# Layer-0 quantised network: its inner half one round later, its first product a round ahead of the gelu, and the bias product over 128 rows

## The reference, cut to what matters

```python
def act_quant(x):
    scale = 127.0 / jnp.clip(jnp.max(jnp.abs(x), axis=-1, keepdims=True), 1e-05)
    q = jnp.clip(jnp.round(x * scale), -128.0, 127.0) / scale
    ...
def bitlinear(x, w, b):
    xq = act_quant(rmsnorm(x))
    wq = weight_quant(w)
    return jnp.einsum('bsd,fd->bsf', xq, wq) + b
h = bitlinear(x, w1, b1)                 # 128 -> 512
h = jax.nn.gelu(h, approximate=False)
return bitlinear(h, w2, b2)              # 512 -> 128
...
x = x + _L0_ffn_ref(_layernorm(x, axis=-1), L0_ffn_w1, L0_ffn_b1, L0_ffn_w2, L0_ffn_b2)
```

## Time and profile before

| | before |
|---|---|
| median of 3 runs | 3581.4 us (3580.28 to 3582.94) |
| the profiled execution | 3559.48 us, its span 3557.9 us |
| mean granted TensorE clock | 0.859 |
| busy share: PE, DVE, ACT, POOL | 79%, 63%, 34%, 12% |
| L601, the bias product: MATMULs, busy, mean of one | 128, 132.6 us, 1137 ns |
| idle time of ACT ahead of the gelu (L639), ended by L601 | 131.5 us in 64 waits |

### The profile page before, as it was taken

How to read it: one execution, slowest core, us unless ns; L and a number is a source line. 1 busy time by engine, 2 the same in 40 slices (tenths; PEclk the granted TensorE clock), 3 DMA queues, 4 the chain that set the end, 5 groups by cost and what they waited for, 6 DMA issues and landing times. The chain is left out here.

```text
span 3557.9 us, 66932 instructions
## 1 busy us (share of the span) xinstructions
PE 2806.2 (79%) x24556; PEld 1846.6 (52%) x24556; DVE 2226.2 (63%) x5515; ACT 1219.6 (34%) x1872; POOL 433.6 (12%) x748
## 2 busy tenths in 40 slices
PE   5867769995999999999987888799852676885356
PEld 4623325663666666666545555466541564664126
DVE  6765548995355555555546777777014557997668
ACT  4535548883000000000016566455320113442230
POOL 0011110000000000000000000034033003442003
PEclk9955559997999999999988888899975778997568
DMA  2010000002121212121200000010322220000001
GB/s 83 27 54 1 1 10 17 15 12 96 60 84 53 91 48 95 48 95 48 95 8 16 10 9 9 2 41 27 90 65 61 60 53 3 0 0 7 0 0 47
DMA packets 88409, 136.96 MB, mean 38 GB/s; under 512 B 42949, under 2 KB 54597, under 8 KB 87242
## 3 DMA queue, kind: packets, MB, share of 16 engines
q1 hardware_dynamic: 80746, 114.75, 10.2%
q0 software_dynamic: 7520, 20.34, 1.9%
HBM read 117.75 MB, written 17.30 MB: 38 GB/s over the span
## 5 line engine op out<-in xcount | busy, mean ns | idle before, releaser
L1424 PE MATMUL banks<-l1f_xe,l1f_w 128*128 128x512 f32 x1024 | 486.7, 598 | 11.1 <-DVE l1f_xe L1623 11.1
L1623 DVE TENSOR_TENSOR l1f_xe<-l1f_hT,l1f_rwb 128x512 f32<-128x512 f32 x256 | 173.3, 692 | 301.0 <-PE banks L1426 278.2
L1426 PEld LDWEIGHTS banks<-l1f_w,l1f_xe 128*128 128x128 f32 x2048 | 269.5, 192 | 123.5 <-issue 123.5
L1629 DVE TENSOR_TENSOR l1f_ae<-l1f_aoT,l1f_rwb 128x512 f32<-128x512 f32 x256 | 172.7, 690 | 160.3 <-PE banks L1454 156.1
L1426 PE MATMUL banks<-l1f_w,l1f_xe 128*128 128x128 f32 x2048 | 270.2, 275 | 0.0
L1424 PEld LDWEIGHTS banks<-l1f_xe,l1f_w 128*128 128x128 f32 x1024 | 176.9, 192 | 141.8 <-issue 127.5
L1454 PE MATMUL banks<-l1f_ae,l1f_w 128*128 128x512 f32 x512 | 225.3, 598 | 1.4 <-DVE l1f_ae L1629 1.4
L1454 PEld LDWEIGHTS banks<-l1f_ae,l1f_w 128*128 128x128 f32 x512 | 97.1, 192 | 118.3 <-issue 116.1
L223 PE MATMUL banks<-consts,l3p_h 128*128 128x128 f32 x64 | 17.8, 433 | 164.6 <-DVE l3p_h L140 164.6
L601 PE MATMUL banks<-l0f_b,l0f_back 4*128 4x512 f32 x128 | 132.6, 1137 | 0.0
L214 POOL COPY x<-xn 128x512 f32 (+1 forms) x16 | 9.8, 610 | 972.7 <-DVE xn L1653 972.7
(11 more groups left out here) (490 smaller groups left out, 6375.5 us busy)
## 6 DMA issues: line engine op xcount, KB each, us to landing
l1f_rwb<-l1f_shares SPq DMA_DIRECT2D x128, 512.0 KB, 4.5
l3p_ctx<-in_ctxT SPq DMA_DIRECT2D x32, 256.0 KB, 3.9
l0a_ctxT<-in_ctxT SPq DMA_DIRECT2D x16, 256.0 KB, 2.7
l2f_sent<-l0f_zero SPq DMA_DIRECT2D x4, 1024.0 KB, 7.0
l1a_ctxT<-in_ctxT SPq DMA_DIRECT2D x16, 256.0 KB, 2.6
l2c_ctxT<-in_ctxT SPq DMA_DIRECT2D x16, 256.0 KB, 2.7
l2e_rows<-l2f_sent SPq DMA_DIRECT2D x16, 256.0 KB, 2.8
l2f_answers<-l2e_y POOLq DMA_DIRECT2D x16, 256.0 KB, 2.7
```

The costliest lines, as they stand in the source:

```text
L1424: pe.matmul(bank, w[:, n, e, :], xe[:, e % NB, :], start=(e == 0), stop=(e == E - 1))
L1426: last = pe.matmul(v_bank[:, D * j:D * j + D], xe[:, e % NB, P * j:P * j + P], w[:, 2, e, :], start=(e == 0 and j == 0), stop=(e == E - 1) ...
L1623: dve.tensor_tensor(xe[:, e % NB, :], hT[:, m, :], rwb[:, m, e, :], ALU.mult).then_inc(s.xe_ready, 1)
L1629: dve.tensor_tensor(ae[:, e % NB, :], aoT[:, m, :], rwb[:, m, e, :], ALU.mult).then_inc(s.ae_ready, 1)
```

## The change

The inner half (from `squares` on) runs one round later on every engine. ACT now starts its round with the gelu of the group whose first product was made in PE's round before, ahead of the copy that releases the next first product. The bias product reads 128 rows of `back` and `b1`, of which rows 4 to 127 are zeros; `back` is cleared once by a new `memset`, and ACT waits for that once (`cleared`) at the start. One wait moves from DVE (`quantise_x`) to ACT (`squares`).

```diff
-        b1 = sb("b1", [TG, TG, F0])
+        b1 = sb("b1", [P, TG, F0])
...
-        back = sb("back", [TG, 2, P])
+        back = sb("back", [P, 2, P])
...
-            pipeline(pe, k.NG, [(1, turn_q), (3, turn_q2), (1, up), (3, down)], unroll=RING4)
+            pipeline(pe, k.NG, [(1, turn_q), (4, turn_q2), (1, up), (4, down)], unroll=RING4)
...
+            act.wait_ge(s.cleared, 2)
...
-                act.copy(back[:, m % 2, :], back_psum)
+                act.copy(back[0:TG, m % 2, :], back_psum)
...
                 wait(act, s.rms2_ready, g - 1)
+                wait(act, s.xn_ready, g - 3)
...
-            pipeline(act, k.NG, [(1, copy_qT), (1, gelu), (3, copy_q2T), (2, scale), (1, squares)], unroll=RING4)
+            pipeline(act, k.NG, [(2, gelu), (1, copy_qT), (4, copy_q2T), (3, scale), (2, squares)], unroll=RING4)
...
             pool.memset(b1[:, :, :].rearrange("p a n -> p (a n)"), 0.0).then_inc(s.cleared, 1)
+            pool.memset(back[:, :, :].rearrange("p a n -> p (a n)"), 0.0).then_inc(s.cleared, 1)
...
-            pipeline(pool, k.NG, [(1, add_bias), (1, rms2), (4, copy_mv)], unroll=RING4)
+            pipeline(pool, k.NG, [(1, add_bias), (2, rms2), (5, copy_mv)], unroll=RING4)
...
                 wait(dve, s.gelu_ready, TG * (g - 3))
-                wait(dve, s.xn_ready, g - 3)
...
-            pipeline(dve, k.NG, [(4, new_x), (2, levels_h), (0, quantise_x), (2, quantise_h)], unroll=RING4)
+            pipeline(dve, k.NG, [(5, new_x), (3, levels_h), (0, quantise_x), (3, quantise_h)], unroll=RING4)
```

## The result

The changed kernel takes 3477.4 us (median of 4 runs, 3471.6 to 3482.1) where the kernel before takes 3581.2 (4 runs, 3580.3 to 3582.9): ratio 0.9709, 95% interval 0.9692 to 0.9726. That is 103.8 us less. Forecast were 101 us and 3480.

The account below looks back on a forecast made before the run. Bound: ACT's 7.42 and PE's 10.26 us in series in an 18.40 us round, then DVE at 12.3. Intervals save 99.9 us, the tail 2, less 1 friction: 3581.4 - 101 = 3480 us, range 3470 to 3510.

Parts of the forecast that it names:

- The ring: Layer 0 round of 18.40 us: PE's product 10.26, last gelu 0.59, ACT's scale, squares and copies 7.42, 0.13 to PE.
- The wait named: ACT's gelu waiting for the bias product, 99.7 us in 48 waits from 258 to 479 us, expected nearly gone.
- the fill: First rounds of layer 0 while the pipeline fills, forecast at 34.4 us in sum before eleven rounds of 12.3.
- The price of the 128-row product: Bias product on PE over 128 rows instead of 4: zero cost at a given clock, from pairs of 2.04 and 2.07 us.
- The clock: TensorE's clock in the layer 0 stretch, 0.50 before, expected to become mixed with mean 0.6 to 0.95.
- the prediction's list of four lengths: Candidates for the new round: ACT 10.2 us, product-gelu-copies chain 11.7, PE 14.6 or 7.6 by clock, DVE 12.13.
- The tail: From the last product's start to the last update, 33.1 us before; 2 us saving forecast through the shorter product.
- 1 us of friction: Allowance deducted from the summed saving in layer 0, leaving 101 us.
- B: Rival: GpSimd's 1.04 us instruction holds DVE's quantise_h, 11 us over eleven rounds, 3491 us; 0.18 with similar friction.
- C: Rival: the clock stays at the lower level and PE bounds rounds at 14.6 us, 3520 us; chance 0.14, or mostly so.
- D: Rival: the bias product costs more over 128 rows than over 4; about 3630 us at twice its price; chance 0.03.
- E: Rival: another wait closes the ring again, rounds stay at 18.4 us, 3581 us; chance 0.03.

Follow-up runs that it names:

- no_swap: Changed kernel with ACT's old order restored, copies ahead of the gelu, the later inner half and 128 rows kept; 3516.0 us, ratio 0.9811 to the kernel before.
- short_dve: Changed kernel with four DVE instructions a group left out, the product of h with two per-token factors; 3454.1 us, ratio 0.9715 to the kernel before.
- lag_only: Changed kernel with the bias product back at 4 rows, the lag and ACT's new order kept; 3501.1 us, ratio 0.9762 to the kernel before.
- rows64: Changed kernel with the bias product over 64 rows in place of 128; 3481.7 us, single run.
- rows_only: Kernel before with only the bias product widened to 128 rows, lags and ACT's order as before; 3511.2 us, ratio 0.9789 to the kernel before.
- late_quantise: Changed kernel with two more DVE bn_stats, results unused, ahead of quantise_h in each round; 3460.0 us, one run.
- before_again: The kernel before, unchanged, run once more for a second profile; 3583.5 us.

## Why the prediction was right, point by point

**The ring and what takes its place.** Right. The wait named is gone, against no row at all. no_swap puts it back by ACT's order alone. The new bound is DVE, as read from the earlier trace rows: 18.40 less its two waits gave 12.13 us, measured are 11.5 in the first rounds and 11.9 to 12.5 later, 11.85 on average against 12.3 forecast. Only two of the eleven (12.5 and 12.3) lie in the 12.1 to 12.6 that I gave as bounds. short_dve shows that it is DVE and not a neighbour of equal length. I had rounded up where nothing asked for it: that is 11 x 0.45 = 5 us of the 6.9 that the intervals are below the forecast (162.8 against 169.7), the rest lies in the fill.

**The price of the 128-row product.** Wrong, to the good side. I compared the durations of one pair, 2.07 and 2.04 us, and set the price at zero. What counts on a busy engine is the distance from one tile's start to the next. It was 2.54 us with 4 rows in all 48 tiles of before. With 128 rows at the same lower level it is 2.11 us, and at the higher level 1.07 where 4, 32 and 64 rows have 1.37. My 1.35 us a tile at the higher level was too long as well, since I took the pair's recorded duration (1.10 us), and the next product starts before that has run out. The timeline of TensorE's weight loads shows where the 0.43 us come from, first before, with its product at 353.02, then after, with its product at 206.78:

```profile
351.01 0.50 PEld L601 LDWEIGHTS banks<-l0f_b,l0f_back 4*128 4x128 f32 x2 [0.44 <-issue]
353.01 0.10 PEld L600 LDWEIGHTS banks<-l0f_w,l0f_qT 128*128 128x128 bf16 x1 [1.50 <-issue]
```
```profile
204.68 0.74 PEld L601 LDWEIGHTS banks<-l0f_b,l0f_back 128*128 128x128 f32 x2
205.93 0.15 PEld L600 LDWEIGHTS banks<-l0f_w,l0f_qT 128*128 128x128 bf16 x1 [0.52 <-issue]
```

Beside products of fewer rows the weights of the next one are loaded at its very start; among products of 128 rows they are loaded 0.85 us ahead. The same holds for the weights of the bias product: at 351.01 with their product, against 204.68 for a product at 205.08. Per group that is 1.7 us at the lower level and 1.2 at the higher. The Trainium skill, page "TensorE: Matmul & The Clock Gate", section "Step-by-step: what each phase is for", says that weight loads are pulled ahead of running products when their row groups don't conflict or when they go to a background buffer, and that the row count doesn't matter for the load's time. The early load at 205.93 agrees; which of its conditions failed for the narrow product no run here shows. That the row count doesn't matter for the load agrees to some 0.05 us: one load of bias weights took 0.28 or 0.33 us with 4 rows and 0.31 or 0.34 with 128, at the lower level.

**The clock.** The forecast (mean 0.6 to 0.95, mixed) was right at 0.80. Its ground was only half right. I had read the earlier trace rows as: 4-row products don't count. What I had made of it for lag_only, that the clock stays at 0.50, was wrong: it is 0.60 with 4 rows once PE is filled. That doesn't refute the reading itself. In PE's round at the lower level (14.6 us) the 4-row pairs take 8.3 and the products of 128 rows 6.3, and those 6.3 us now come every 12.8 us in place of every 18.4. Rows do matter: 0.61 and 0.71 for 32 and 64 rows, with the same pitch (single runs), and 0.80 for 128, where the pitch is shorter too; how much of that last step is the rows and how much the closer products, no run separates. PE's idle stretches go with the clock as well: rows64 runs at the lower level in the round after each wait shown above, and the tail of the changed kernel stands at 0.51. The page of the Trainium skill weighed in the prediction, "TensorE: Matmul & The Clock Gate", section "Why this matters for your kernels", ties the clock to a busy TensorE without gaps; lag_only, 97% busy at 0.60, and before, 79% at 0.50, are not at the full clock that it alone would give; the falls after the waits of rows64 agree with it.

**The sum and its parts.** The two parts are worth 73.2 us (rows_only) and 78.5 us (lag_only) of the phase when made alone, and 104.8 together: the second stops at DVE's floor, as the prediction's list of four lengths says. The tail was the term with the wrong sign: 2 us saved were forecast, 2.0 were lost. rows_only, which has the faster product but not the lag, saves 4.8 there, so the product's share was right; the lag costs 36.9 - 30.1 = 6.8 us, and I had put that down as "some". The last product itself is shorter, as forecast: from its first start to its last end 5.8 us (367.46 to 373.24) against 10.2 (479.20 to 489.43). But none of that comes through, as ACT's rows of the kernel after show:

```profile
376.36 2.39 ACT L640 ACTIVATE l0f_h<-banks,l0f_sx 128x512 f32<-128x512 f32 x4
...
382.10 2.56 ACT L654 ACTIVATE l0f_h<-l0f_h,l0f_sh 128x512 f32<-128x512 f32 x4 [1.54 <-DVE l0f_sh L757]
384.56 0.61 ACT L647 ACTIVATE l0f_sq<-l0f_h 128x512 bf16<-128x512 f32 x1
```

The last gelus stand behind the scale and the squares of older groups and end at 378.75, 11.3 us after the last product's start (11.0 before); then the scale waits 1.54 us for DVE's factor. The squares of the last group start 17.1 us after that product's start, against 15.1 before, and that is the 2.0 us; from there to the start of the last update both kernels take the same 18.0. I had counted the chain of the last group and not the parts of older groups that stand in it. In all, the intervals are 106.8 us shorter where 99.9 were forecast, and no 1 us of friction can be told apart in them. So the total came within 3 us of the forecast because the errors are small and partly cancel.

**The rivals.** B didn't happen: DVE's quantise_h kept its 1.22 us. In the kernel after the two meet as foreseen, and it is GpSimd's short addition that grows, from 0.23 to 0.92 us, ahead of a power that still takes 1.04:

```profile
340.43 1.22 DVE L763 TENSOR_SCALAR l0f_q<-l0f_h 128x2048 bf16<-128x2048 f32 x1
340.81 0.92 POOL L685 TENSOR_SCALAR l0f_sh<-l0f_sh 128x4 f32<-128x4 f32 x1 [8.53 <-ACT l0f_sq L647]
341.81 1.04 POOL L687 TENSOR_TENSOR l0f_sh<-l0f_sh,l0f_half 128x4 f32<-128x4 f32 x1
```

late_quantise let GpSimd go first in some rounds, and GpSimd paid again. The Trainium skill, page "SBUF — State Buffer", section "Who interferes with whom", gives the ports that GpSimd shares with DVE's fast modes to whoever is first, for the whole instruction. The 0.92 us agree with it, and the 2.07 us of the earlier trace rows do; the power of 4 elements a row that started first doesn't, and the measurement decides for it. Why, no run shows. C didn't happen: with PE filled the clock did not stay low even with 4 rows (lag_only, 0.60). D had the sign of the pitch wrong. E didn't happen; no_swap, where the ring is closed by ACT's order, shows what it would have cost beside the wide product: rounds of 13.7 us, not 18.4.

**The offset.** I carried the 21.9 us between the profiled execution and the median as untouched by the change. For the medians that held, and before_again says what it is: mostly the l2h part of layer 2. For the profiled execution it did not: forecast were 3458.5 us, measured 3471.6, as this one has 103.6 us of l2h where the profile before had 83.8. The spread of layer 3's attention (299 to 316 us) is a risk of the size of my error bars that I had not weighed; that before and after happen to have 301.8 and 299.3 there is luck.

## What to carry to other kernels

When two engines' times add up to the round, look for the one instruction that stands behind the release of its own input; moving it a round ahead is worth at most the shorter of the two, and no more than down to a third engine's own length, which can be read off before as round less waits (here 12.1 us, measured 11.85). Price a product on TensorE by the distance between starts, not by its duration, and try a narrow product between wide ones with its rows filled up by zeros: here it was faster at either clock. When a phase gets faster and the total doesn't, compare the phases' lengths one by one before blaming the edit: here a phase far behind, at a lower clock, took back 13 us.

## What the runs showed of the hardware that I had not expected

- Products of 4, 32 or 64 rows between 128-row ones: 2.54 us (lower level) and 1.37 us (higher) from tile to tile, against 2.11 and 1.07 with 128 rows.
- A 128x512 float32 multiplication on GpSimd took 1.85 us and a 128x512 rounding to bf16 1.93 us, where its addition took 1.25 to 1.27; on DVE the rounding takes 0.43. The multiplication ran in part beside a DVE instruction.
- One part of layer 2 takes 84 or 104 us, the same in all runs made together and both on one chip at different times. The attention of layer 3 took 299 to 316 us; by what, is open.
